# Routed windows and two-branch attention, image by image: head and router moved between the attention tiles

## The reference

```
q_c, k_c, v_c = split(xs @ qkv_cmp_w)                    # per pixel
k_cmp = mlp(unfold(k_c, 4x4, stride 2) + pos)            # 225 keys: layer 2048 -> 256, gelu, 256 -> 128
v_cmp = mlp(unfold(v_c, 4x4, stride 2))
attn_cmp = softmax(q_c @ k_cmp * SCALE)                  # 1024 x 225, 4 heads
idx = top_k(sum of attn_cmp over heads and pixels, 16)
k_s, v_s = the 16 chosen 4x4 blocks                      # 256 keys
out_slc = softmax(q_s @ k_s * SCALE) @ v_s
out_win = attention inside 7x7 windows (25 per image, with a bias table)
g = sigmoid(gelu(xs @ gate_w1) @ gate_w2)
out = g0 * out_cmp @ p0 + g1 * out_slc @ p1 + g2 * out_win @ p2
```

## Time and profile before

| | us |
|---|---|
| median of 3 runs | 871.69 (871.59 to 872.61) |
| the profiled execution | 869.9 |
| its span, first to last instruction | 868.0 |

### The profile page before, as it was taken

How to read it: one execution, slowest core, us unless ns; L and a number is a source line. 1 busy time by engine, 2 the same in 40 slices (tenths; PEclk the granted TensorE clock), 3 DMA queues, 4 the chain that set the end, 5 groups by cost and what they waited for, 6 DMA issues and landing times.

```text
span 868.0 us, 17389 instructions
## 1 busy us (share of the span) xinstructions
PE 666.8 (77%) x5028; PEld 503.4 (58%) x5029; DVE 551.5 (64%) x1772; ACT 427.9 (49%) x1231; POOL 243.3 (28%) x411
## 2 busy tenths in 40 slices
PE   2997767699776779978767898776742399999953
PEld 1694344569534346964434597443441399998952
DVE  4435888776498868649787765887964144444434
ACT  1326536433753634356355325733711288787852
POOL 5100040130434001124400211631013355555540
PEclk9998998999999889999988999896985599999985
DMA  9800000000000000001000000100032122222236
GB/s 319 232 1 1 1 4 1 26 24 1 28 23 5 1 25 25 1 17 34 5 1 1 1 25 4 47 7 24 0 114 51 50 65 61 67 65 63 63 108 233
DMA packets 34220, 39.59 MB, mean 46 GB/s; under 512 B 11246, under 2 KB 26720, under 8 KB 33888
## 3 DMA queue, kind: packets, MB, share of 16 engines
q1 hardware_dynamic: 28592, 27.74, 10.6%
q0 software_dynamic: 4416, 9.00, 3.1%
q10 hardware_dynamic: 1152, 2.10, 0.7%
HBM read 25.39 MB, written 14.50 MB: 46 GB/s over the span
## 4 chain that ended last, share of the span: by engine, by line
PE 49%; DVE 26%; issue 9%; DMA 6%; POOL 5%; ACT 4%; SPq 1%; POOLq 1%; DVEq 0%; ACTq 0%
PE ps L1293 7%; PE ps L1506 6%; PE ps L1345 6%; DVE nmx L910 6%; DVE r_P L920 5%; PE ps L1287 4%; PE ps L1312 4%; PE ps L1615 3%; PE ps L1369 3%; PE ps L1599 3%; DMA R<-xs_d 3%; PE ps L1336 3%; ACT r_P L685 2%; POOL xs_d L625 2%; DMA kbdw<-z_d 2%
## 5 line engine op out<-in xcount | busy, mean ns | idle before, releaser
L685 ACT ACTIVATE r_P<-ps,nmx 128x225 f32<-128x225 f32 (+1 forms) x192 | 85.9, 465 | 44.1 <-DVE nmx L910 44.1
L827 ACT ACTIVATE R<-ps,R 128x128 f32<-128x128 f32 x292 | 83.5, 368 | 46.4 <-PE ps L1599 46.3
L1287 PE MATMUL ps<-ident,r_P 128*128 128x128 f32 (+1 forms) x384 | 62.0, 310 | 54.1 <-DVE r_P L920 45.4
L1287 PEld LDWEIGHTS ps<-ident,r_P 128*128 128x128 f32 (+1 forms) x384 | 48.6, 165 | 85.5 <-DVE r_P L920 69.5
L625 POOL DMA_INDIRECT xs_d<-pay,pos x64 | 62.3, 974 | 124.9 <-DVE pos L1090 106.7
L910 DVE TENSOR_REDUCE nmx<-ps 128x4 f32<-128x900 f32 (+1 forms) x64 | 73.5, 1154 | 24.9 <-PE ps L1369 24.9
L659 POOL DMA_INDIRECT z_d<-R x72 | 69.4, 964 | 68.7 <-DVE R L1258 46.0
L1369 PE MATMUL ps<-kbd,qT 64*128 64x450 f32 (+1 forms) x256 | 76.1, 697 | 6.7 <-ACT kbd L802 5.1
L1599 PE MATMUL ps<-R 128*128 128x128 f32 x584 | 79.0, 279 | 0.0
L1615 PE MATMUL ps<-fw_sb,R 128*128 x576 | 77.9, 278 | 0.0
L558 POOL TENSOR_TENSOR rstd<-vpe,minus_half 128x8 f32<-128x8 f32 x8 | 13.3, 1658 | 212.7 <-DVE vpe L885 212.7
(11 more groups left out here) (217 smaller groups left out, 1323.4 us busy)
## 6 DMA issues: line engine op xcount, KB each, us to landing
R<-xs_d SPq DMA_DIRECT2D x76, 65.0 KB, 1.8
kbdw<-z_d SPq DMA_DIRECT2D x8, 512.0 KB, 5.0
x_sb<-x SPq DMA_DIRECT2D x4, 512.0 KB, 3.4
w1k_sb<-w1k SPq DMA_DIRECT2D x1, 2048.0 KB, 10.0
w1v_sb<-w1v SPq DMA_DIRECT2D x1, 2048.0 KB, 14.7
fw_sb<-fw SPq DMA_DIRECT2D x1, 2048.0 KB, 10.5
fw_sb<-fw SPq DMA_DIRECT2D x4, 512.0 KB, 11.0
t_d<-r_P SPq DMA_DIRECT2D x4, 512.0 KB, 2.6
```

The lines of the kernel that those rows point to most:

```text
L685: last = sc.activation(Pb[t % NRING][:, h, 0:m], bank(ph, name)[:, (h % 2) * m:(h % 2) * m + m], ACT.Exp, bias=nmx[:, t % NRING, h:h + 1], ...
L827: last = sc.activation(hT[:, r % 2, c, :], hid(r)[:, C * c:C * c + C], ACT.Gelu, bias=wx[:, r, O_B1 + c:O_B1 + c + 1])
L1287: last = tr(bank(ph, name)[0:m, k * j:k * j + k], src, ident[0:k, 0:k])
```

## The change

The seam is taken apart, and its pieces go between the tiles.

- **Compressed tiles** of image b also hold, a piece per tile: the turning and normalising of the image b + 1 and its block keys and values; the window queries and window values of image b itself; and of image b - 1 the router's input, logits, choices and ranks.
- **Windows** hold the key layer of b + 1, eight matmuls first and then four per group; **selected tiles** hold the value layer of b + 1, four matmuls per tile, its gates, second key layer and queries, and the gated biases of b (VectorE).
- **Seam**: the projection by tokens, `combine`, both steps of normalising `t`, the payload, and of the next image only the first scores, the window keys, the second value layer with the gates, and the selected queries.
- In all tile loops the scores of tile t + 1 are issued in step t, behind the turning of tile t - 2; the turned chunks are copied out three tiles behind the scores (`F_LAG`), at the start of a step.
- **PSUM**: scores have banks 0 to 3, turned chunks 4 and 5, what is between the tiles 6 and 7 (in the compressed loop); each PSUM bank is named in a table written out by hand.
- **Buffers**: two `x_tok`, an own `t_tok`, `ocT`, `owT`, `qTs`, `hk`, `hv`, `vs_sb`. For the room, the expert weights lie over the first layers' weights and are loaded after the last value layer, in the third seam; `kbdw` and `kbd` hold two head planes instead of four, so that window scores are two matmuls of 64 rows and 98 columns for each window, and not one of 128 rows and 196.
- Queries and block values go from VectorE to ScalarE (the first image's values excepted). Key blocks are written with two instructions on 128 partitions, not four on 32. The copy of the image (`x_res`) falls away.
- **GpSimd**: the windows' layout of b + 1 and then the scatter of b - 1 come behind the window stage of b. **SyncE**: `t` of the last image isn't stored and loaded again.

The core of the diff (names with `@{b}` are the image's):

```diff
-NRING = T_LAG + 1
+F_LAG = 3
+NRING = 3
 PSLOT = 6
 O_LAG = 6
 PW_LAG, OW_LAG = 2, 3
 W_EARLY = 2
-PJ_FIRST = 4
...
+    def scores(s, t, b):
+        for k in range(2):
+            put(2 * (t % 2) + k, f"S{s}{t}{'ab'[k]}@{b}")
+    def turned(s, t, b):
+        for k in range(2):
+            put(4 + k, f"T{s}{t}{'ab'[k]}@{b}")
...
+        extra = around((6, 7))
+        for t in range(NT + F_LAG):
+            if 0 <= t - T_LAG < NT:
+                turned("c", t - T_LAG, b)
+            if t + 1 < NT:
+                scores("c", t + 1, b)
+            extra(*compressed_extras(b, t))
...
+def compressed_extras(b, t):
+    h, prev = b + 1, b - 1
+    following = {0: ("xt0", "xt1"), 5: ("xh0", "xh1"), 6: ("kc0", "kc1"), 7: ("vc0", "vc1")}
+    before_it = {1: ("tt0", "tt1"), 3: ("rt",), 8: ("rk",)}
+    own = {2: ("qw0", "vw0"), 3: ("vw1",), 4: ("vw2", "qw1"), 8: ("vw3", "qw2"), 9: ("vw4", "vw5"), 10: ("vw6",)}
+    names = [f"Oc0@{b}"] if t == O_LAG + 1 else []
+    if h < B:
+        names += [f"{n}@{h}" for n in following.get(t, ())]
+    if prev >= 0:
+        names += [f"{n}@{prev}" for n in before_it.get(t, ())]
+    return names + [f"{n}@{b}" for n in own.get(t, ())]
...
+        w1_sb = sb("w1_sb", [128, E * WPK])
+        w1k_sb = w1_sb[:, 0:2 * C * NPOS].rearrange("p (s n) -> p s n", s=NPOS)
+        w1v_sb = w1_sb[:, 2 * C * NPOS:4 * C * NPOS].rearrange("p (s n) -> p s n", s=NPOS)
+        fw_sb = w1_sb[:, :].rearrange("p (e n) -> p e n", e=E)
...
+            def compressed_tiles(b):
+                h, prev = b + 1, b - 1
+                for t in range(NT + F_LAG):
+                    if t >= F_LAG:
+                        first_chunk(b, "c", t - F_LAG)
+                    if t < NT:
+                        maxima(b, "c", t, NB)
+                    if 1 <= t <= NT:
+                        divide(b, "c", t - 1, NB)
+                    if t == 1 and h < B:
+                        for i in range(2):
+                            dve.wait_ge(*copied(f"xt{i}@{h}"))
+                        row_sums(x_tok[h % 2])
+                    if t == 2 and h < B:
+                        row_variances(EPS_C)
+                    if t == 3 and h < B:
+                        if prev >= 0:
+                            dve.wait_ge(*filled(f"tt1@{prev}"))
+                        normalised(2 * b + 1, x_tok[h % 2], xhat_tok, xhat_tok_ready)
+                    if t == 3 and prev >= 0:
+                        router_logits(prev)
+                    if t == 4 and prev >= 0:
+                        router_maxima(prev)
+                    if t == 5 and prev >= 0:
+                        router_choices(prev)
+                    if t == 6 and prev >= 0:
+                        router_counts(prev)
+                    if t == O_LAG + 1:
+                        branch_output(b, "c", 0, ocT)
+                    if t == 8 and prev >= 0:
+                        ranks(prev)
+                    if t == 9 and prev >= 0:
+                        rows_of_picks(prev)
...
+            def compressed_tiles(b):
+                h, prev = b + 1, b - 1
+                for t in range(NT + F_LAG):
+                    if 0 <= t - T_LAG < NT:
+                        turned_probabilities(b, "c", t - T_LAG, (M0, M1))
+                    if t + 1 < NT:
+                        scores(b, "c", t + 1, NB)
+                    if t == O_LAG + 1:
+                        pe.wait_ge(*copied(f"gv@{b}"))
+                        branch_output(b, "c", 0, (M0, M1))
+                    if t == 0 and h < B:
+                        image_by_tokens(h)
+                    if t == 1 and prev >= 0:
+                        router_input(prev)
+                    if t == 2:
+                        window_projection(b, "qw", 0, 0)
+                        window_values(b, 0)
+                    if t == 3:
+                        if prev >= 0:
+                            router_logits(prev)
+                        window_values(b, 1)
+                    if t == 4:
+                        window_values(b, 2)
+                        window_projection(b, "qw", 0, 1)
+                    if t == 5 and h < B:
+                        for i in range(2):
+                            pe.wait_ge(*copied(f"qs{i}@{b}"))
+                        normalised_image(h)
+                    if t == 6 and h < B:
+                        block_projection(h, "kc", 1)
+                    if t == 7 and h < B:
+                        block_projection(h, "vc", 2)
+                    if t == 8:
+                        if prev >= 0:
+                            ranks(prev)
+                        window_values(b, 3)
+                        window_projection(b, "qw", 0, 2)
+                    if t == 9:
+                        window_values(b, 4)
+                        window_values(b, 5)
+                    if t == 10:
+                        window_values(b, 6)
...
+            def window_stage(b):
+                h = b + 1
+                if h < B:
+                    key_layer(h, range(8))
...
+                    if h < B and g < W_EARLY + 6:
+                        key_layer(h, range(8 + 4 * (g - W_EARLY), 12 + 4 * (g - W_EARLY)))
...
+            def selected_tiles(b):
+                h = b + 1
+                for t in range(NT + F_LAG):
+                    if 0 <= t - T_LAG < NT:
+                        turned_probabilities(b, "s", t - T_LAG, (128, 128))
+                    if t + 1 < NT:
+                        scores(b, "s", t + 1, 256)
+                    if t < NT and h < B:
+                        value_layer(h, range(4 * t, 4 * t + 4))
+                    if t == T_LAG - 1:
+                        pe.wait_ge(vselT_ready, b + 1)
+                        transposes(f"vt@{b}", [vselT[:, 128 * a:128 * a + 128] for a in range(2)], 128, 128)
+                    if t == O_LAG + 1:
+                        pe.wait_ge(*copied(f"vt@{b}"))
+                        pe.nop(nofuse=True)
+                        branch_output(b, "s", 0, (128, 128))
+                    if t == NT and h < B:
+                        gate_hidden(h)
+                    if t == NT + 1 and h < B:
+                        compressed_keys(h)
+                    if t == NT + 2 and h < B:
+                        block_projection(h, "qc", 0)
...
+            def seam(b):
+                h = b + 1
+                branch_output(b, "s", 1, (128, 128))
+                if h < B:
+                    first_scores(h)
                     pe.wait_ge(xwin_ready, h + 1)
+                    for i in range(len(WPARTS)):
+                        window_projection(h, "kw", 1, i)
+                pe.wait_ge(*copied(f"Oc1@{b}"))
+                pe.wait_ge(*copied(f"Os1@{b}"))
+                pe.wait_ge(*copied(f"OW{NGRP - 1}@{b}"))
+                for t in range(NT):
+                    branches_by_tokens(b, t)
+                if h < B:
+                    compressed_values_and_gates(h)
+                    slc_queries(h)
+                else:
+                    router_input(b)
+                    router_logits(b)
+                    ranks(b)
```

1671 lines of the change are left out of this document (897 added, 774 removed).

## The result

| | median (us) | range | runs |
|---|---|---|---|
| kernel before | 872.14 | 871.59 to 872.61 | 4 |
| changed kernel | 840.66 | 840.26 to 842.45 | 4 |

The ratio is 0.964 (0.963 to 0.966): 31.5 us less. The forecast was 820 with a range of 800 to 850, so the direction and the range held and 20.7 us of the gain didn't come. The profiled execution of the changed kernel has a span of 838.5.

What follows compares the result with a forecast made beforehand. TensorE was taken to bound the seam and VectorE the tiles. Opening 65, compressed tiles 38 + 43 + 43, windows 3 x 34.5, selected 3 x 38.5, seams 3 x 24, last image 98 and end 238 sum to 816.0; 819.7 us, range 800 to 850.

Steps and rivals of the forecast that it cites:

- opening: Start of the run: loses window values and queries, gains selected queries that cover a wait; 65 us against 72.88.
- compressed tiles, images 1 to 3: Compressed stage with additions on VectorE and TensorE, longer engine added tile by tile: 38 us first image, 43 second and third.
- windows: Window stage, TensorE loses the query projection and gets the key layer, 31.2 us busy: 34.5 us against 30.7.
- selected tiles: Selected stage with the value layer and gated biases added, TensorE the bound at 37.5 busy: 38.5 us against 28.1.
- seam: Between images: work moved out leaves a dependency chain that sums to 23.7, taken as 24 us against 67.9.
- last image up to its seam: Last image, no next head, gets the third's router and gated biases, loses window query projection: 98 us against 89.7.
- third rival: Tile loops: bank round trip closes in one tile, half the excess exposed, 2.5 us a tile: 900 us, slower; chance 0.07.
- second rival: Extras' banks 6 and 7, refilled only after ScalarE's late copies, cost 0.8 us in each tile: 845 us; chance 0.19.
- rival 1: Full cover and full clock in the three attention stages, 5.5 us an image less on three images: 805 us; chance 0.14.
- tail: End of the window stage: selected projection, VectorE's flips and last groups, some 12 us after TensorE reaches 21.
- The rule on the clock: TensorE in the filled stages: activity releases the throttled clock, so they would run at 2.4 GHz throughout.
- The tests that I named: Profile signs: seam 24 us, VectorE or TensorE above 85% in compressed tiles, gapless selected tiles, clock near 1.0, ScalarE-copy waits.

Runs made afterwards that it cites:

- a: Changed kernel with ScalarE's copy of the turned second chunk right behind the same step's exponentials, compressed tiles only: 850.6 us, ratio 0.943 to the kernel before on that chip.
- m: f with ScalarE's copies of the window values made twice, the first to an unread buffer: 800.4 us, ratio 0.919 to the kernel before.
- d: Changed kernel with the next image's first maximum taken in the seam before the normalising, its exponentials behind ScalarE's seam work: 860.7 us, ratio 0.959 to the kernel before.
- f: Changed kernel with the edits of c and d together: 800.5 us, ratio 0.917 to the kernel before, 0.952 of the changed kernel.
- c: Changed kernel with all copies out two tiles later instead of three, on VectorE and ScalarE, in both tile stages: 837.8 us, ratio 0.929 to the kernel before.
- b: Changed kernel with VectorE's first-chunk copy behind the same step's division, in compressed and selected tiles: 859.3 us, ratio 0.950 to the kernel before on that chip.
- after2: The changed kernel run again word for word, as base of a later group: 841.0 us, ratio 0.963 to the kernel before.
- j: Changed kernel with ScalarE's copies of the window values made twice, the first to an unread buffer: 856.6 us, ratio 0.985 to the kernel before.
- g: Changed kernel with the next tile's scores issued ahead of the turning of two tiles back on TensorE: 829.7 us, ratio 0.950 to the kernel before.
- first group: Runs of a, b, c and d on one chip, beside the kernel before, which took 900.9 us there; the changed kernel itself did not run in it.
- h: Changed kernel with every indirect store of an image's rows issued twice, the second to an unread buffer: 866.2 us, ratio 0.992 to the kernel before.

## Why the prediction was right, and where it was off

Forecast against measured span, by the terms of its sum:

| term | forecast | measured | difference |
|---|---|---|---|
| opening | 65 | 63.9 | -1.1 |
| compressed tiles, images 1 to 3 | 38 + 43 + 43 | 44.3 + 47.5 + 50.8 | +18.6 |
| windows | 3 x 34.5 | 30.2 + 30.8 + 30.2 | -12.3 |
| selected tiles | 3 x 38.5 | 40.3 + 40.7 + 40.7 | +6.2 |
| seam | 3 x 24 | 22.5 + 22.6 + 22.6 | -4.3 |
| last image up to its seam | 98 | 114.1 | +16.1 |
| end | 238 | 237.2 | -0.8 |
| span | 816.0 | 838.5 | +22.5 |

**Compressed tiles: the step that failed.** The additions were sized well (VectorE 37.6 forecast, 35.6 measured; TensorE 36.9, 39.3 with part of it at the low clock), and adding the longer engine tile by tile is nearly what the kernel does once the copies are out of the way: a takes 38.6, 43.3 and 43.6 for the forecast 38, 43 and 43. What failed is the sentence against the third rival, "scores stand a tile ahead and the copies out three tiles behind, so two turns of the ring lie between". The copies three tiles behind are no slack. The turned chunks have one pair of banks, so a copy that comes a step later is a bank that comes free a step later. The second rival had the right pair of engines and the right price (0.8 us a tile forecast, 0.6 to 1.0 measured, and its 845 lies near the 840.7), but the wrong banks: TensorE has no wait for ScalarE in front of window values or keys in the second image, and by m the copies of the window values cost nothing where the turned chunk goes first. That 845 lies so near is in part luck, since errors in other stages lie in the 840.7 too.

**Why the total held.** The range held by luck in part: 40.9 us too little in compressed tiles, selected tiles and the last image stand against 18.5 us too much in the other terms. Two slips of the working change nothing: VectorE's work in the compressed tiles adds up to 37.4 us and not 37.6, and rival 1's 5.5 us on three images are 16.5 and not 15.

**The first tile** is the second miss in the compressed tiles. At each image's start VectorE takes the first maximum only after normalising, gates and payload, though the scores have been there for 20 us. The last image's start on TensorE, L1594 being scores:

```profile
479.39 1.03 PE L1594 MATMUL ps<-kbd,qT 64*128 64x450 f32 x4
489.31 2.72 PE L1594 MATMUL ps<-kbd,qT 64*128 64x450 f32 x4 [8.90 <-ACT r_P L783]
```

I priced the seam by its chain and took the next stage from its first maximum, and never asked what TensorE does in between: it waits 4.5 to 8.9 us for banks 0 and 1, and comes back at the low clock, 2.72 us for scores of 1.03. d and f move the maximum into VectorE's own wait for GpSimd's root. f is 2 to 4 us an image shorter than c by it; the rest of the idle is filled by the next waits, in the second image of f 2.5 us for ScalarE's copy of the selected queries before the next image is turned, and 1.1 us for VectorE's division.

**Windows: right engine, too long.** TensorE is the bound, 28.4 of 30.8 busy, where I had 31.2 busy and a tail. One part is the window scores, by groups of instructions with busy time and mean ns of one, in the kernel before and in the changed one:

```profile
L1321 PE MATMUL ps<-kbdw,qwT 128*49 128x196 f32 x34 | 4.0, 339 | 0.0
```

```profile
L1636 PE MATMUL ps<-kbdw,qwT 64*49 64x98 f32 x68 | 2.6, 253 | 0.0
```

Each window's scores are now two matmuls of half the rows and half the columns, and take less in all; I had carried them over as unchanged. The other part is the clock, 1.00 for 0.85. The selected projection, where my tail begins, in the second image:

```profile
267.22 1.13 PE L1827 MATMUL ps<-r_P,qkvs_sb 128*128 128x256 f32 x4 [0.56 <-DMA r_P<-xblk]
```

The tail itself came as forecast: from this projection to the stage's end at 279.55 it is 12.3 us for my 12. But TensorE is there 18.5 us after the stage's start and not 21, and I had taken 1.5 us more than the sum of the two. This error hid half of the one in the tiles.

**Selected tiles**: TensorE 36.4 for my 37.5, but with 4.3 us idle. "TensorE is the bound" was so, "without gaps" was not: the tiles stand 3.9 us apart, and 5.2 where VectorE's gated bias stands ahead of its copy (scores at 286.8, 290.7 and 295.9 in the second image). With the copy ahead (b, c, f) the stage is 37.6 to 38.1 in the first image, near the 38.5 that I forecast.

**Seam**: each step of the chain as read (combination 7.7 for 7.3, statistics to the first normalised row 4.5 for 4.4), except that the first projected tile stands at 5.9 for 7.5: the branch output of 3.64 us in the earlier trace rows is now 1.93, at the full clock.

**Last image**: of +16.1, 11 are in its compressed tiles (47.0 for 36), 3.6 in the selected (36.6 for 33), 1.5 in the windows (30.5 for 29). I had carried it over from before with VectorE as its bound. It has fewer fillers than the others, so TensorE idles more, and its clock was 0.88, 0.70 and 0.79.

**Opening and end** were right, and so was the nil for the expert weights' later load and for the scatter under the selected tiles (40.7 us with it, 40.3 without, in the first image).

**The rule on the clock** (Trainium skill, TensorE: Matmul & The Clock Gate, Part 1: The HAM clock gate): with the stages filled, the granted clock in windows and selected tiles is 1.00 for 0.85 and 0.93, as the rule has it. It isn't near 1.00 in the compressed tiles (0.96, 0.93, 0.85). In the second image the low part is the start, behind the idle; in the third the rest isn't at full speed either (0.91 from 356.00 on), and why isn't shown:

```profile
201.27:215.00 13.73, 10.92 (x48) 6.51 (x48) 12.66 (x47) 11.82 (x41) 1.64 (x1) 0.75 0.01 2
215.00:248.73 33.73, 28.34 (x198) 18.35 (x199) 22.91 (x99) 19.62 (x62) 0.84 (x1) 1.00 0.00 1
```

The tests that I named gave this: seam 22.6 for 24; no engine above 85% in the compressed tiles, which was the sign of what went wrong; and TensorE waiting for ScalarE's copies, but those of the turned chunks.

## What to carry to other kernels

A later copy out is slack only where there are banks for it. With one pair for a stream, the copy belongs at the first place in its engine's queue where its data can be there, ahead of all filler; filler that is moved into a pipelined loop goes behind the loop's own copies on every engine, not only on the one that was full. And before a stage is priced by the sum of its engines, walk its first iteration: what was put at the end of the queue in the stage before is what it starts with.

## What the runs showed of the hardware

**An idle may cost twice.** The same 220 records of TensorE in the last image's compressed tiles took 33.8 us busy in after2, at a clock of 0.90, and 39.4 in j, at 0.79; the stages took 46.2 and 52.3. The low clock isn't particular to j's copies: the same stage took 49.8 us in g at 0.77 and 49.7 in a at 0.73. That a wait of half a microsecond a tile costs more than it lasts, by way of the clock, fits these rows but isn't shown; why the clock fell in one kernel's last image and not in another's stays open.

**Indirect stores and standstills of three engines on one chip.** In the first group each of the four kernels took 46 to 50 us for the selected tiles of the second and third image, with a scatter beside them, and 37.6 to 40.3 in the first image, which has none. In the last image they took 40 to 41 us for 36.4 in after2, and its windows, at whose end the scatter begins, 35 to 37 for 30.5 in the changed kernel of the result. There VectorE, ScalarE and TensorE stand still together, and no instruction of the kernel releases them, while GpSimd goes on issuing a store every 1.26 us. From c_both_copy, the second image; "remote" is idle time that nothing in the profile's own events ends:

```profile
286.19 0.60 ACT L798 ACTIVATE R<-ps 128x512 f32<-128x512 f32 x1 [6.49 <-remote]
...
286.84 1.11 PE L1483 MATMUL ps<-ident,r_gh 128*128 128x128 f32 x4 [4.83 <-issue]
...
290.55 1.23 DVE L1060 TENSOR_REDUCE nmx<-ps 128x4 f32<-128x1024 f32 x1 [7.22 <-remote]
```

The only transfers of that stage, by queue (packets, MB, share of 16 engines):

```profile
q0 software_dynamic: 512, 1.07, 6.8%
q8 instruction: 2, 0.03, 0.3%
q14 instruction: 3, 0.02, 0.2%
```

A guess is that the three engines stood without instructions, because their few packets were held up beside the scatter's 512. It isn't shown, and this speaks against it: on the other chips the stage has the same two kinds of packets and no stall, and twice the stores cost nothing there (h). What differs on that chip stays open; the kernel before took 3% longer on it too, and its trace there wasn't kept, so whether it has the same standstills isn't known.
